# A two-layer gated transformer block: summed squares folded on VectorE before TensorE sums them, and one turning of tokens moved behind a weighing

## The reference

```
x = x + tanh(g_xattn[0]) * causal_attention(layernorm(x), ctx, ctx)        # 16 heads of 32
x = x + tanh(g_ffn[0])   * ffn0(layernorm(x))
x = x + tanh(g_xattn[1]) * cross_attention(layernorm(x), ctx; q, k_img, v_img, o weights)
x = x + tanh(g_ffn[1])   * ffn1(layernorm(x))
```

```
gate, up = split(x @ Wgu.T)          # 2048 each
h  = silu(gate) * up
hn = h * rsqrt(mean(h * h) + eps)    # mean over the 2048 hidden values of a token
y  = hn @ Wp.T
```

## Time and profile before

| | us |
|---|---|
| median of three runs | 1142.21 |
| lowest and highest | 1140.67, 1143.71 |
| the profiled execution | 1139.14 |
| its span, first to last instruction | 1137.4 |

### The profile page before, as it was taken

One profiled execution on the slowest core, in us unless ns is written; L12 is line 12 of the kernel. 1 busy time (PEld: TensorE's weight loads), 2 busy tenths in 40 slices (PEclk: granted clock), 3 DMA queues, 4 the chain that ended last, 5 costly groups with the idle time before them and its releaser, 6 DMA issues.

```text
span 1137.4 us, 25529 instructions
## 1 busy us (share of the span) xinstructions
PE 1096.0 (96%) x10342; PEld 669.3 (59%) x10450; DVE 832.7 (73%) x1440; ACT 567.2 (50%) x918; POOL 74.5 (7%) x180
## 2 busy tenths in 40 slices
PE   8899999999999999999999999899999999999998
PEld 3455555556777777777777655455454545454543
DVE  5688888788767648566565667886868778777795
ACT  3676667766433333333333452455554637372654
POOL 0000000000000000000001012010101010101010
PEclk9899999999999999999999999999999999999999
DMA  9565555443212011021010201101010100000001
GB/s 361 185 194 169 181 193 156 154 122 122 67 38 65 20 38 37 20 75 28 29 57 20 84 2 38 37 2 56 1 57 1 57 1 30 10 11 11 10 10 38
DMA packets 29268, 79.24 MB, mean 70 GB/s; under 512 B 3041, under 2 KB 3297, under 8 KB 28897
## 3 DMA queue, kind: packets, MB, share of 16 engines
q1 hardware_dynamic: 29152, 77.61, 21.0%
HBM read 65.02 MB, written 12.58 MB: 68 GB/s over the span
## 4 chain that ended last, share of the span: by engine, by line
PE 89%; issue 3%; ACT 3%; DVE 2%; DMA 2%; SPq 1%; POOL 0%; ACTq 0%; DVEq 0%; POOLq 0%
PE bank L587 10%; PE bank L586 10%; PE bank L692 10%; PE bank L672 9%; PE bank L545 9%; PE bank L795 8%; PE bank L425 5%; PE bank L825 5%; PE bank L783 5%; PE bank L745 3%; PE bank L764 3%; PE bank L477 2%; PE bank L498 2%; PE bank L510 2%; PE bank L450 2%
## 5 line engine op out<-in xcount | busy, mean ns | idle before, releaser
L586 PE MATMUL bank<-ARENA,W 128*128 128x256 f16 x1024 | 227.3, 273 | 0.7 <-issue 0.7
L587 PE MATMUL bank<-ARENA,W 128*128 128x256 f16 x1024 | 227.2, 273 | 0.0
L1002 ACT ACTIVATE ARENA<-bank 128x512 f32<-128x512 f32 (+3 forms) x143 | 92.9, 687 | 81.3 <-PE bank L425 32.6
L545 PE MATMUL bank<-ARENA 128*128 128x512 f32 x256 | 119.4, 609 | 1.4 <-DMA ARENA<-in_wkv 1.4
L795 PE MATMUL bank<-W,ARENA 128*128 128x512 bf16 x493 | 116.6, 382 | 2.5 <-issue 0.7
L692 PE MATMUL bank<-ARENA 128*128 128x512 f32 x256 | 116.9, 600 | 0.0
L672 PE MATMUL bank<-W,ARENA 128*128 128x512 bf16 x472 | 114.6, 379 | 2.2 <-issue 0.2
L586 PEld LDWEIGHTS bank<-ARENA,W 128*128 128x128 bf16 x1024 | 100.0, 98 | 19.5 <-issue 1.3
L587 PEld LDWEIGHTS bank<-ARENA,W 128*128 128x128 bf16 x1024 | 100.1, 98 | 17.9
L1002 ACT ACTIVATE ARENA<-ARENA 128x512 f16<-128x512 f32 x64 | 40.3, 630 | 136.1 <-DVE ARENA L1585 129.6
L1585 DVE SCALAR_TENSOR_TENSOR ARENA<-bank,ARENA 128x512 f32<-128x512 f32 x64 | 48.0, 750 | 76.4 <-PE bank L587 73.5
(11 more groups left out here) (179 smaller groups left out, 1766.5 us busy)
## 6 DMA issues: line engine op xcount, KB each, us to landing
W<-in_w SPq DMA_DIRECT2D x48, 512.0 KB, 4.0
ARENA<-in_w SPq DMA_DIRECT2D x24, 512.0 KB, 3.6
kv_store<-ARENA SPq DMA_DIRECT2D x32, 256.0 KB, 3.8
W<-kv_store SPq DMA_DIRECT2D x15, 512.0 KB, 4.0
ARENA<-in_ctxT SPq DMA_DIRECT2D x8, 512.0 KB, 3.8
X<-in_x SPq DMA_DIRECT2D x8, 512.0 KB, 5.8
ARENA<-in_ctx SPq DMA_DIRECT2D x8, 512.0 KB, 5.9
out<-X SPq DMA_DIRECT2D x16, 256.0 KB, 2.0
```

Source lines behind the costliest of these rows:

```text
L545: mm = pe.matmul(bank, bufA["KT"][:, b % 2 * KD + k, t * P:(t + 1) * P], W[:, k, :], start=(k == 0), stop=(k == KD - 1 and what == 1))
L586: pe.matmul(bank[:, i * S:(i + 1) * S], W0[:, at:at + P], xt_half(b, 0)[:, k, :], start=(k == 0), stop=False)
L587: mm = pe.matmul(bank[:, i * S:(i + 1) * S], W0[:, at:at + P], xt_half(b, 1)[:, k, :], start=False, stop=(k == KD - 1))
L1002: return act.activation(to, src, ACT.Copy)
```

## The change

The first edit folds the two halves of `acc` on VectorE, right behind the last addition of squares (step 7) of each batch, and lets TensorE sum 128 x 256 instead of 128 x 512. The wait of `b_sum_squares` goes from `b_acc` to a new semaphore `b_fold`. The second edit exchanges two neighbouring calls of TensorE's list at the end of turn 2: the last weighing of batch 1 stands before the turning of batch 3's tokens. The lists of the other engines and the order within the banks stay as they are.

```diff
@@ names of semaphores
-    ... b_sq b_acc b_ss ...
+    ... b_sq b_acc b_fold b_ss ...
@@ TensorE, b_sum_squares
                 pe.wait_ge(sem, value)
-                pe.wait_ge(s.b_acc, 7 * (b + 1))
-                for t in range(TB):
-                    for i in range(2):
-                        mm = pe.matmul(to[:, 2 * t:2 * t + 2], bufB["acc"][:, b % 2, i * S + t * P:i * S + (t + 1) * P], keep["ones"][:, 0:2],
-                                       start=(i == 0), stop=(i == 1))
+                pe.wait_ge(s.b_fold, b + 1)
+                for t in range(TB):
+                    mm = pe.matmul(to[:, 2 * t:2 * t + 2], bufB["acc"][:, b % 2, t * P:(t + 1) * P], keep["ones"][:, 0:2], start=True, stop=True)
                 mm.then_inc(s.b_ss, 1)
@@ TensorE, end of turn 2
             d_turn_q(0)
+            c_weigh(1, 3)
             c_turn_x(3)
-            c_weigh(1, 3)
@@ VectorE
+            def b_fold(b):
+                acc = bufB["acc"][:, b % 2, :]
+                v.wait_ge(s.b_acc, 7 * (b + 1))
+                v.tensor_tensor(acc[:, 0:S], acc[:, 0:S], acc[:, S:2 * S], ALU.add).then_inc(s.b_fold, 1)
@@ VectorE, step p of batch b
                     if p:
                         b_add_square(b, p)
+                    if p == 7:
+                        b_fold(b)
```

More of the change, by code:

```diff
@@ L43 @@
     a_ab a_sg a_gs a_s a_r a_abs a_kv a_kvr
-    b_ve b_rstd b_xn b_xt b_xh b_xl b_g b_gu b_sg b_h b_sq b_acc b_ss b_me b_inv b_hh b_hl b_pr b_xy b_neg b_w1
+    b_ve b_rstd b_xn b_xt b_xh b_xl b_g b_gu b_sg b_h b_sq b_acc b_fold b_ss b_me b_inv b_hh b_hl b_pr b_xy b_neg b_w1
     c_ve c_rstd c_xn c_xt c_xtr c_kss c_kinv c_kn c_kt c_ktr c_sc c_scr c_mhl c_mt c_mtr c_st c_ex
```

## The result

The changed kernel took 1134.47 us (median of 10 runs, 1132.91 to 1137.02) against 1141.63 us of the kernel before in the same comparison: ratio 0.994, 95% interval 0.9929 to 0.995. Two later comparisons gave 0.9952 (0.9935 to 0.9969) and 0.9951 (0.9935 to 0.9966). Forecast were 1139.2 us, a ratio of 0.9973, and a range down to 1136.4. The direction was right; the path part of the forecast, 3.06 us, is 43% of the 7.2 us between these medians and some 55% of the 5.5 and 5.6 us of the later two. The two profiled executions lie only 4.92 us apart (1139.14 and 1134.22), their spans 4.93 (1137.36 and 1132.43).

What follows compares the result with a forecast made beforehand. TensorE, busy 96% of the span, was taken as the bound, with VectorE costing only where TensorE waits for it. Terms -2.84 + 0.45 - 0.67 = -3.06 us, laid on the 1142.21 us median, gave 1139.2 us; range 1136.4 to 1141.9.

Steps and rivals of the forecast that it cites:

- the path part of the forecast: Whole kernel: seven shorter sums, delay at the eighth batch and the swap, -2.84 + 0.45 - 0.67 = -3.06 us.
- TensorE's saving per sum: Sum of squares on TensorE: four instructions instead of eight, 0.405 us saved each time, seven times 2.84 us.
- The fold hidden at seven boundaries: Feed-forward stage, VectorE: the fold delays what follows by 0.45 us, hidden by 1.7 us slack at the worst boundary.
- rival (4): Feed-forward batch boundaries: VectorE sets the bound, each of 8 batches costs 0.45 us; +2.9 us, 1145.1 us; chance 0.03.
- The eighth batch: Behind the last batch the fold delays the next stage's first maxima and the scores: +0.45 us, no gain from the shorter sum.
- The swap: End of turn 2: scores 1.86 us ahead, but the value product waits for VectorE's last division, so 0.67 us gained.
- By the rows alone the stretch stays as it is and the sum stands: Late in the kernel, near 1116 us: the half-clock stretch, costing some 1.2 us, was taken to remain unchanged.
- The base: The -3.06 us was laid on the median of the runs shown, 1142.21 us, giving 1139.2 us.
- Rival (1): Late half-clock stretch goes or another comes, by 1.2 us: 1138.0 or 1140.4 us; chance 0.20, in halves.
- Rivals (2): VectorE isn't late behind the eighth fold, or the swap gives the whole 1.86 us: 1138.3 or 1138.0 us; chance 0.09.
- (3): Turn 2: the swap gives nothing because the weighing's bank comes free late: 1139.8 us; chance 0.09.
- (5): Sum of squares: four instructions take as long as eight; only swap and eighth fold left, -0.2 us: 1142.0 us; chance 0.04.

Runs made afterwards that it cites:

- before, three gaps filled: Kernel before plus twelve, five and seven unused bf16 products in three places where TensorE waits: 1138.16 us, ratio 0.9973.
- path gains and gaps filled: Changed kernel, eighth batch unfolded, third weighing divided before normalisation in turn 2, six, five and seven unused products in three waits: 1133.1 us, ratio 0.9931 against before.
- the fold alone: Kernel before plus VectorE's fold into its own buffer; TensorE waits for it but sums both halves as before, turn 2 in old order: 1141.16 us, ratio 1.001.
- leaving the eighth out: Changed kernel with the last batch not folded but summed by the four products of before: 1135.59 us, ratio 0.9959 against the kernel before.
- one gap filled: Kernel before plus twelve unused bf16 products of 128x512 in TensorE's 2.79 us wait in turn 2: 1138.43 us, ratio 0.9979.
- changed again: The changed kernel as it is, measured twice more against the kernel before: 1134.83 us (0.9952) and 1134.27 us (0.9951).
- the first of the last two: Changed kernel without the eighth batch's fold and with the third weighing divided before the normalisation in turn 2, no extra work: 1134.68 us, ratio 0.995 against before.

## Why the prediction was wrong

All runs of four kernels for which the clock is known, with the mean of the time and of the granted clock:

| kernel | runs | mean us | mean clock |
|---|---|---|---|
| before | 58 | 1140.89 | 0.9930 |
| before, three gaps filled | 7 | 1137.89 | 0.9953 |
| changed | 25 | 1135.32 | 0.9949 |
| path gains and gaps filled | 5 | 1133.06 | 0.9962 |

The clock of a run comes in steps (0.990, 0.991, 0.993, 0.994 and so on, 0.0015 apart): one half-clock stretch more or less. Runs of the kernel before at 0.994 have a mean of 1139.93 us (21 runs), at 0.993 of 1140.96 (17), at 0.991 of 1142.43 (13). A line fitted through the 161 runs of all kernels, with an offset for each kernel, gives 0.88 (standard error 0.04) us for 0.001 of clock, so 1.3 us a step; single stretches behind 60 us cost 1.3 to 1.7 us at matched instructions. The steps aren't even, though: the changed kernel's runs have a mean of 1133.59 us at 0.997 (7 runs), 1134.23 at 0.995 (9) and 1137.37 at 0.994 (6), so one step is worth 0.6 us and the next 3.1. Why is open.

The fourteen profiles have half-clock stretches between 60 us and the end at three places only: in turn 2 (in one of the three profiles whose wait there is 2.8 us long, in none of the eleven others), at the wait of 1.28 us near 1053 (in four of the twelve in which it isn't filled) and at the wait of 1.60 us near 1116 (in three of the same twelve). The two profiles with all three waits filled have none.

Step by step:

- **TensorE's saving per sum**: forecast 0.405, measured 0.44, seven times -3.11 instead of -2.84 us. I had spread the 0.81 us over 8 instructions; the loads of the sum are 0.11 us apart, and four of those went. Small, in the right place, and the seven fall where they should.
- **The fold hidden at seven boundaries**: right. No idle time of TensorE appeared before any sum, with the fold in the changed kernel or alone; rival (4), the slower one, falls. It took 0.43 us against 0.42.
- **The eighth batch**: right to 0.01 us, +0.46 us forecast as +0.45, and confirmed from both sides, by the fold alone and by leaving the eighth out.
- **The swap**: the mechanism right, the size 0.43 instead of 0.67 us. I let the reciprocal start before the multiply ahead of it had ended. But `c_weigh` waits on VectorE for `s.c_pvr` at 4 b + g, that is for the end of that multiply and its signal: 0.14 us after the end instead of 0.08 before it, 0.22 in all. The wait stands in the kernel's function. I read the order of the instructions there and not their waits. The end of the last multiply at 724.88 us, which the forecast takes from the earlier trace rows, isn't among them; this is its line in the profile of before:

```profile
724.46 0.42 DVE L1658 TENSOR_TENSOR ARENA<-bank,ARENA 128x256 f32<-128x256 f32 x1
```

- **"By the rows alone the stretch stays as it is and the sum stands"**: this is the step that failed. I took the 2.79 us of idle time in turn 2 to cost no clock, because the one profile shows 1.00 there. Of the three profiles with that gap one has the clock at 0.50 in it and behind it, at a cost of 1.33 us. Filling the gap with unused work in the kernel before gave 2.3 us (0.9 to 4.0), filling it and two others 3.1 us with no run below a clock of 0.995. The swap cuts the one long wait into 0.79 and 1.71 us with the weighing between them, and none of the seven profiles of kernels with the swap and no filler has a stretch there. I had read the number of stretches from one execution, and it was one of the kernel before's luckier ones: its clock is 0.994 where the mean of 58 runs is 0.9930. I had the spread of the runs in hand, in steps of 1.5 us, and used it only to widen the range on both sides. It says that stretches come and go, and an edit that takes idle time from TensorE takes away chances to lose one.
- **The base**: the difference of -3.06 us was laid on the median of three runs, 1142.21 us; the ten runs of the comparison have 1141.63. Of the 4.7 us between forecast and result 0.6 come from there, 2.5 are gain beyond the path that all runs together bear out (5.57 between the means above, less 3.06), and 1.6 are the luck of the first comparison.
- **Rival (1)** named the thing but priced it as a coin toss of one stretch either way, at 1.2 us worked out from fifteen products; at matched instructions the stretch near 1118 cost 1.68. The swing isn't even: the share of time in such stretches fell, by 0.0019 of mean clock. The rule of the Trainium skill (TensorE: Matmul & The Clock Gate, "What's actually happening"), that the monitor runs free of the kernel, agrees with the runs: one kernel, executed again, has its stretches at different places, at 1052 and 1117 or nowhere behind 60 us.
- **Rivals (2), (3) and (5)** fall with the rows above: the scores after the eighth batch came 0.46 us later and the value product waited 1.71 us for VectorE, the swap gave 0.43 us and not nothing, and the four instructions took 0.50 us where eight took 0.95.

What the parts come to: of 5.57 us between the means of before and changed, 3.08 are the path by matched instructions, 0.29 the stall at 817 us, and the clock is worth 1.65 (the fitted line leaves 3.92, standard error 0.21, at equal clock). About 0.55 us is left open. The kernel with one gap filled, whose path is the old one, also lies 0.4 (standard error 0.3) and the one with three gaps 1.0 (0.35) below what its clock would say. One could think that the mean clock undercounts, because it weighs a step of the first 60 us, where TensorE waits for data and ScalarE anyway, like a late one. The profiles don't bear that out: four of them (changed, changed again, the fold alone, the first of the last two) have the early stretch one step shorter, and at 286 us they are on average 1.1 us ahead of the ten others, with a spread as large as that within each group. How much of the clock's 1.65 us comes from turn 2 isn't shown either. It can't be more than the 1.3 us that a stretch costs there, and in the profiles one in three had it. Between two kernels whose gaps are all filled, three gaps filled and the last kernel, the means are 1137.89 - 1133.06 = 4.83 us apart (standard error 0.5), and the path and the stall come to 3.08 + 0.29 + 0.46 + 0.70 = 4.53: there the account closes within the error.

Open is also why the kernel before reached a clock above 0.995 in one of 58 runs, while the changed one has 0.997 in 7 of 25.

## What to carry to other kernels

An idle gap of the matrix engine has two prices: its length, if it is on the path, and the chance that the clock is halved behind it. A reordering that splits or fills a long gap can be worth more than the critical path says, and a filler of unused matmuls is a cheap test for it; with gains near the spread of the runs it needs many runs, and the clock of each says more than the median. And before a difference of one profile is laid on a median, look where that profile's clock and time stand among the runs. Where a step counts an instruction as starting right behind another on the same engine, its waits have to be read as well: a wait on the engine's own semaphore took a third of the gain here.

## What the runs showed of the hardware

- The same kernel differed by 4.7 us between two profiled executions, 4.5 of them at two half-clock stretches (mean clock 0.997 and 0.991), with the same instructions in the same order.
- A wait of TensorE of 2.80, 1.60 or 1.28 us was followed by half clock in some profiles and not in others: in one of three, three of twelve and four of twelve.
- Adding twelve products of 128x512 in a wait of 2.79 us made the kernel faster by 0.21% (0.08 to 0.35%).
- An f32 product of two columns costs TensorE's queue 0.22 us (two loads 0.11 us apart); a 128x256 f32 addition of VectorE costs 0.43 us.
- A stall of 0.28 us between two bf16 products at 817 us is in the four profiles of kernels without the fold in VectorE's program, which runs for the last time 170 us earlier, and in none of the ten with it; no cause is shown.
- The wait for a result of VectorE's maxima before the next scores is charged as "issue" in these profiles (0.42 and 0.88 us); the change of 0.46 us under the fold alone shows whose it is.
